# Row maxima of the second cross-attention: four heads at a time in row groups of the array, into one buffer of four banks

## The reference

```python
def _L1_xattn_ref(qkv, y):
    N_HEADS = 16
    bs, width, length = qkv.shape
    ch = width // N_HEADS
    q = qkv.reshape(bs * N_HEADS, ch, length)
    k = v = y.reshape(bs * N_HEADS, ch, -1)
    scale = 1.0 / math.sqrt(math.sqrt(ch))
    weight = jnp.einsum('bct,bcs->bts', q * scale, k * scale)
    weight = jax.nn.softmax(weight.astype(jnp.float32), axis=-1).astype(weight.dtype)
    a = jnp.einsum('bts,bcs->bct', weight, v)
    return a.reshape(bs, -1, length)
...
x = x + jnp.tanh(g_xattn[1]) * _L1_xattn_ref(_layernorm(x, axis=-1), ctx_2048)
```

## Time and profile before

| | |
|---|---|
| Median of three runs | 1993.25 us (1988.57 to 2001.61) |
| The profiled execution's own time | 1990.66 us |
| Its span, first to last instruction | 1988.8 us |
| Granted clock of TensorE, mean over the span | 0.926 of full speed |
| Busy in the span: TensorE matmuls, VectorE, ScalarE, GpSimd | 1719.1, 1290.5, 777.5, 829.1 us |
| Reductions of the maxima (L1257) | 512, 484.2 us |
| Matmuls of the maxima (L1383) | 1024, 315.0 us |

### The profile page before, as it was taken

How to read it: one execution, slowest core, us unless ns; L and a number is a source line. 1 busy time by engine, 2 the same in 40 slices (tenths; PEclk the granted TensorE clock), 3 DMA queues, 4 the chain that set the end, 5 groups by cost and what they waited for, 6 DMA issues and landing times. The chain is left out here.

```text
span 1988.8 us, 23904 instructions
## 1 busy us (share of the span) xinstructions
PE 1719.1 (86%) x8103; PEld 871.0 (44%) x8134; DVE 1290.5 (65%) x1649; ACT 777.5 (39%) x1275; POOL 829.1 (42%) x369
## 2 busy tenths in 40 slices
PE   5999999994656777899999998999999986989996
PEld 2444444442444543444444444444444323444443
DVE  3668989857898775766666665666666413565553
ACT  1211212113444533565655555655565554011010
POOL 0012222012554426577776676777767660000000
PEclk9999999996788876999999998999999996999999
DMA  8030312302000045143344444443332302000002
GB/s 320 9 114 20 89 44 66 124 34 82 1 0 0 0 104 142 39 105 92 87 98 105 105 105 106 105 94 78 89 86 70 71 1 87 1 0 0 0 0 85
DMA packets 83551, 137.19 MB, mean 69 GB/s; under 512 B 16606, under 2 KB 53490, under 8 KB 82678
## 3 DMA queue, kind: packets, MB, share of 16 engines
q1 hardware_dynamic: 83446, 135.84, 25.0%
HBM read 70.73 MB, written 8.66 MB: 40 GB/s over the span
## 5 line engine op out<-in xcount | busy, mean ns | idle before, releaser
L1257 DVE TENSOR_REDUCE c_piece_max<-c_unit 128x1 f32<-128x804 f32 x512 | 484.2, 990 | 280.4 <-PE c_unit L1383 277.1
L1342 ACT ACTIVATE c_prob<-c_scores 128x512 f32<-128x512 f32 (+1 forms) x832 | 472.2, 596 | 365.6 <-PE c_scores L1400 356.4
L1192 POOL TENSOR_TENSOR c_prob_sum<-c_prob_sum,c_prob 128x2048 f32<-128x2048 f32 x96 | 439.7, 4580 | 68.3 <-ACT c_prob L1342 64.3
L1400 PE MATMUL c_scores<-c_queries,c_keys 98*128 98x512 f32 (+1 forms) x832 | 358.1, 451 | 30.9 <-ACT c_prob L1342 16.6
L1383 PE MATMUL c_unit<-c_khigh,c_qdiag 128*128 128x402 f32 x1024 | 315.0, 393 | 23.3 <-DVE c_piece_max L1257 12.5
L1383 PEld LDWEIGHTS c_unit<-c_khigh,c_qdiag 128*128 128x128 f32 x1024 | 189.0, 204 | 175.9 <-DVE c_piece_max L1257 92.3
L1409 PE MATMUL c_out<-c_prob,c_VT 128*32 128x512 f32 (+1 forms) x1664 | 228.4, 629 | 22.1 <-issue 22.1
L1400 PEld LDWEIGHTS c_scores<-c_queries,c_keys 98*128 98x128 f32 (+1 forms) x832 | 158.0, 193 | 186.6 <-ACT c_prob L1342 132.3
L525 PE MATMUL a_S<-a_ctxT,a_xnT 128*128 128x401 f32 x512 | 188.9, 513 | 7.2 <-ACT a_prob L490 3.9
L555 PE MATMUL a_o<-a_ctx,a_probT 128*128 128x512 f32 (+1 forms) x416 | 181.2, 592 | 0.0
L1192 POOL TENSOR_TENSOR c_prob_sum<-c_prob 128x2048 f32<-128x2048 f32 x16 | 72.5, 4534 | 137.0 <-ACT c_prob L1342 137.0
(11 more groups left out here) (204 smaller groups left out, 2099.1 us busy)
## 6 DMA issues: line engine op xcount, KB each, us to landing
c_keys<-c_khigh SPq DMA_DIRECT2D x128, 200.2 KB, 3.0
c_k<-in_keys SPq DMA_DIRECT2D x16, 801.0 KB, 6.3
c_keys<-c_k SPq DMA_DIRECT2D x64, 200.2 KB, 3.0
a_ctx<-in_ctx SPq DMA_DIRECT2D x12, 1024.0 KB, 5.4
c_VT<-in_values SPq DMA_DIRECT2D x16, 768.0 KB
a_ctxT<-in_ctxT SPq DMA_DIRECT2D x12, 802.0 KB, 4.8
c_queries<-c_qhigh SPq DMA_DIRECT2D x128, 64.0 KB, 2.6
a_weights<-in_L_ffn_weight SPq DMA_DIRECT2D x3, 1408.0 KB, 13.6
```

Of the source, the lines that this page charges most:

```text
L1192: nc.gpsimd.tensor_tensor(psum4[:], a[:], prob[(j * MC + c) % RING][:], ALU.add).then_inc(sums_taken, 2 if i == 1 else 1)
L1257: nc.vector.tensor_reduce(piece_max[j % 2][:, k // 2, k % 2:k % 2 + 1], U[bank(unit)][:, :, 0:PIECE], axis=AX.XY, op=ALU.max).then_inc(uni ...
L1342: nc.scalar.activation(prob[(j * MC + c) % RING][0:w, h, :], STp[h % 2][0:w, :], ACT.Exp, scale=SCALE).then_inc(exp_done, 1)
L1400: nc.tensor.matmul(STp[h % 2][0:w, :], K[p][:, h, c * P:c * P + w].bitcast(F32R), Q[p][:, h, :].bitcast(F32R), start=True, stop=True).then ...
```

## The change

A unit of the maxima is now four matmuls, one for each head, for one group of 128 queries and one piece of 402 keys. Each works on the 32 partitions of its head with a `tile_position` in its own group of 32 rows of the array, and writes to its own bank. The unit fills all four banks, which before were two buffers of two, so the next unit may be issued only when VectorE has read this one. VectorE reduces 4 x 402 elements to four columns at once. A block has 16 units instead of 32 pairs (a stream of 17 with rows instead of 33), spread over the same 48 gaps. The zero-padded copies `QZ`, their fills on GpSimd, their transfers on SyncE's queue and the semaphore for them are gone; the matmuls read `qhigh` itself, so ScalarE's writing of `qhigh` for block n waits until the last unit of block n - 2 has been issued and done.

```diff
-        PAIRS = H * TB * 2
+        PIECES, PER = len(STARTS), H
+        PAIRS = H // PER * TB * PIECES
         UNITS = PAIRS + 1
-        AHEAD, ROWS_AT = PAIRS // 2, 8
+        AHEAD, ROWS_AT = PAIRS // 2, 4
...
-        QZ = [sb(f"c_qdiag{j}", [P, H, D]) for j in range(2)]
...
-        piece_max = [sb(f"c_piece_max{j}", [P, H * TB, 2]) for j in range(2)]
+        piece_max = [sb(f"c_piece_max{j}", [P, H, TB, PIECES]) for j in range(2)]
...
-        U = [ps(f"c_unit{j}", [P, 2, 512]) for j in range(2)]
+        U = ps("c_unit", [P, PER, 512])
...
-                if more:
-                    load_diagonal(g + 2, j % 2)
...
-            steps.link(pool.memset(QZ[0][:], 0.0))
...
-            steps.link(pool.memset(QZ[1][:], 0.0))
...
-                nc.vector.tensor_reduce(piece_max[j % 2][:, k // 2, k % 2:k % 2 + 1], U[bank(unit)][:, :, 0:PIECE], axis=AX.XY, op=ALU.max).then_inc(unit_read, 1)
+                h0, t, piece = part(k)
+                nc.vector.tensor_reduce(piece_max[j % 2][:, h0:h0 + PER, t, piece], U[:, :, 0:PIECE], axis=AX.X, op=ALU.max).then_inc(unit_read, 1)
...
-                    act.wait_ge(diag_loaded, (n - 1) * DIAGS)
+                    act.wait_ge(unit_full, FULL0 + place(n - 2, PAIRS - 1) + 1)
...
-                h, t, half, o = k // (2 * TB), k // 2 % TB, k % 2, j % 2
+                (h0, t, piece), o = part(k), j % 2
                 if k == 0:
-                    pe.wait_ge(diag_loaded, (n + 1) * DIAGS)
+                    pe.wait_ge(qhigh_ready, n + 1)
                     pe.wait_ge(khigh_ready, n + 1)
-                pe.wait_ge(unit_read, place(n, k) + 1)
-                for e in range(2):
-                    at = STARTS[2 * half + e]
-                    last = nc.tensor.matmul(U[bank(unit)][:, e, 0:PIECE], QZ[o][:, h, t * P:(t + 1) * P].bitcast(F32R), khigh[o][:, at:at + PIECE], start=True, stop=True)
+                pe.wait_ge(unit_read, place(n, k) + UNITS0)
+                at = STARTS[piece]
+                for e in range(PER):
+                    head = slice((h0 + e) * CH, (h0 + e + 1) * CH)
+                    last = nc.tensor.matmul(U[:, e, 0:PIECE], qhigh[o][head, t * P:(t + 1) * P], khigh[o][head, at:at + PIECE],
+                                            start=True, stop=True, tile_position=((h0 + e) * CH, 0))
                 last.then_inc(unit_full, 1)
```

More of the change, by code:

```diff
@@ L1023, in cross_attention_1 @@
         stacked = sem("c_stacked")
-        diag_loaded = sem("c_diag_loaded")
         unit_full = sem("c_unit_full")
@@ L1042, in cross_attention_1 @@
         FINS = 1
-        STACKS, ROWS, DIAGS = 16 * H * 6, 16 * H, 16 * H
+        STACKS, ROWS = 16 * H * 6, 16 * H
         EXPS0, PV0, UNITS0, FULL0, SCORES0 = 2, RING, 2, 1, 1
@@ L1087, in unit_stream, with part @@
             return stream
[L1089 to L1094, removed]
+        def part(k):
+            return k // (TB * PIECES) * PER, k // PIECES % TB, k % PIECES
         block = stack.enter_context(nc.Block())
@@ L1106, in load_values @@
                 sp.dma_start(VT[j][0:ML, MC - 1, :], src[:, (MC - 1) * P:M, :].rearrange("o p k -> p (o k)")).then_inc(v_loaded[j], 16)
[L1108 to L1114, removed]
             load_keys(0, 0)
             load_keys(1, 1)
-            sp.wait_ge(consts_ready, 3)
-            load_diagonal(0, 0)
-            sp.wait_ge(consts_ready, 4)
             def slot(g, j, main, nxt, more, later):
@@ L1260, in maximum @@
                     dve.wait_ge(unit_read, UNITS0 + place(n, k) + 1)
-                    nc.vector.tensor_reduce(nmax[:].rearrange("p h t -> p (h t)"), piece_max[j % 2][:], axis=AX.X, op=ALU.max, negate=True).then_inc(nmax_ready, 1)
+                    nc.vector.tensor_reduce(nmax[:], piece_max[j % 2][:], axis=AX.X, op=ALU.max, negate=True).then_inc(nmax_ready, 1)
             def keep_rows(unit):
@@ L1266, in keep_rows @@
                 dve.wait_ge(unit_full, FULL0 + rows_place(n) + 1)
-                nc.vector.tensor_copy(nrow[:], U[bank(unit)][0:2 * H, 0, :]).then_inc(unit_read, 1)
+                nc.vector.tensor_copy(nrow[:], U[0:2 * H, 0, :]).then_inc(unit_read, 1)
                 dve.wait_ge(unit_read, UNITS0 + rows_place(n) + 1)
@@ L1388, in rows @@
                 pe.wait_ge(nparts_ready, n + 1)
-                pe.wait_ge(unit_read, rows_place(n) + 1)
+                pe.wait_ge(unit_read, rows_place(n) + UNITS0)
                 for t in range(TB):
-                    last = nc.tensor.transpose(U[bank(unit)][0:2 * H, 0, t * P:(t + 1) * P], nparts[:, t, :, :].rearrange("p h a -> p (h a)"), ident[:])
+                    last = nc.tensor.transpose(U[0:2 * H, 0, t * P:(t + 1) * P], nparts[:, t, :, :].rearrange("p h a -> p (h a)"), ident[:])
                 last.then_inc(unit_full, 1)
@@ L1436, in slot @@
                         rows(unit) if unit[0] == "rows" else pair(unit)
-                    pe.wait_ge(consts_ready, 7)
+                    pe.wait_ge(consts_ready, 5)
                     for h in range(H):
```

## The result

The change made the kernel slower: median 2099.2 us (2094.27 to 2102.86) against 1992.7, a ratio of 1.053 (95% interval 1.048 to 1.057). The forecast was 2014 us: slower, as measured, but by a fifth of the measured step. The profiled execution has a span of 2099.1 us against 1988.8, 110 more.

What follows compares the result with a forecast made beforehand. TensorE's in-order queue was taken as the bound. 5 (prologue) + 3 (block 0's slot) + 13 slots x (0.3 + 0.8) + 0.5 (slot 14) = 22.8 us on 1990.66 gave 2013.5, with the median's offset 2014 us; range 1955 to 2070.

Steps and rivals of the forecast that it cites:

- Order and bound: Second cross-attention blocks: TensorE's in-order queue is the bound, busy 49.2 of 52.6 us a block at 2.4 GHz.
- Four matmuls in row groups: Units of the maxima: four matmuls overlap in 0.2 us, about 0.4 us from unit to next score with mode changes.
- The rival in which they don't overlap: Units' four matmuls hold 0.74 us, every interval grows by 0.54, 9 us a block, 2162 us in all; chance 0.08.
- The single buffer: Maxima's buffer: TensorE must wait for VectorE's read, so at least 2.44 us from unit to unit, setting eight intervals a block.
- The walk through a block: Sum of the intervals from unit to unit in one block at full clock: 52.9 us, against 52.6 before.
- The clock: Turns of the blocks: longer idle brings two stretches at low clock at nearly every turn, another 0.8 us a block.
- The rival with the clock: Blocks: units with idle between them leave the clock low longer, two further stretches a block, 2046 us; chance 0.17.
- the 57 that the prediction named as a sign of being wrong: Reciprocals, one a block: expected 53 to 55 us apart; under 51 or over 57 would show the forecast wrong.
- Block 0's slot: Slot of block 0, 24 intervals instead of 48 pairs: 64.2 us against 62.2 before, with a slow start +3.
- The prologue: Block 0's units at 1.2 GHz: 2.7 us each, start 2.2 us earlier, the rest of the maxima 5 us later.
- The rival "no price for the change of mode": Weight loads stay hidden: unit holds 0.25, scores around it 0.23, 49.2 us a block, 1964 us in all; chance 0.19.

Runs made afterwards that it cites:

- the gaps filled: The changed kernel with whole-array matmuls added between two scores, or a score and a unit, that had nothing between them: 2084 us, ratio 1.042 to before.
- the padded units on the single buffer: The changed kernel with zero-padded copies over all 128 rows in place of row groups, four-bank single buffer kept: 2144 us, ratio 1.076 to before.
- the run with two heads: The changed kernel with row groups kept but two heads a unit, 32 units, into two buffers of two banks: 2089 us, ratio 1.044 to before.
- the run with seven: The changed kernel with each unit's four matmuls issued seven times over into the same banks: ratio 1.164 to before, 70.7 us a block.

## Why the prediction was wrong

**Order and bound** held: TensorE's queue is still the busiest (83% of the span), and VectorE, GpSimd and ScalarE have the busy time per block that they had the earlier trace rows.

**Four matmuls in row groups** held. I took 0.4 us from unit to score, and it is 0.38. The rival in which they don't overlap is out.

**The single buffer** held: 2.40 us from unit to unit against 2.44.

**The walk through a block** was 1.8 us short. At full clock the 13 intervals from the fourth on take 38.9 us by the starts of their reductions, where I had 37.1. With my figures for the other four that makes 54.7 us a block against 52.9. Two terms were too small. The score between two modes holds 0.43 in place of 0.34 or 0.33. The larger one is the loop through ScalarE, 1.18 us for two scores, which the walk charged only in "s s s out". It also sets "s s out s" (2.87 us against 2.44), the interval behind the rows (1209.40 to 1213.20, so 3.80 against 3.12) and "s s den sum out s" (1218.81 to 1223.40, so 4.59 against 4.15), three intervals that make some 1.5 of the 1.8 us, about 1.3 of it by scores that wait for an exponential. In "s s out s" the third row starts 1.19 us after the first:

```profile
1189.59 0.73 PE L1384 MATMUL c_scores<-c_queries,c_keys 98*128 98x512 f32 x2
1190.25 0.45 PE L1366 MATMUL c_unit<-c_khigh,c_qhigh 32*128 32x402 f32 x4
1190.78 0.98 PE L1384 MATMUL c_scores<-c_queries,c_keys 98*128 98x512 f32 x2
1191.70 1.06 PE L1393 MATMUL c_out<-c_prob,c_VT 128*32 128x512 f32 x8
1192.69 0.49 PE L1384 MATMUL c_scores<-c_queries,c_keys 98*128 98x512 f32 x1
1193.12 0.46 PE L1366 MATMUL c_unit<-c_khigh,c_qhigh 32*128 32x402 f32 x4
```

The comparison that made me trust the walk could not have shown this: the 3.22 us "measured" are 1255.84 to 1259.06, the same rows from which its prices were read, so the sum had to come out. These reductions open and close the stretch of 38.9 us (timeline of VectorE, after), and its row by engine follows:

```profile
1185.04 1.83 DVE L1239 TENSOR_REDUCE c_piece_max<-c_unit 128x4 f32<-128x1608 f32 x1 [0.59 <-PE c_unit L1366]
...
1223.91 1.83 DVE L1239 TENSOR_REDUCE c_piece_max<-c_unit 128x4 f32<-128x1608 f32 x1 [2.76 <-PE c_unit L1366]
...
1185.04:1223.91 38.87, 34.57 (x210) 11.76 (x210) 23.74 (x17) 20.71 (x38) 26.73 (x11) 1.00 0.09 19
```

**The clock** is the step that failed: "another 0.8 a block". I let the low clock come only at the turns, as a longer version of the dips of before. Slots 1 to 13 now take 60.7 us a block on average, 6.0 over the 54.7 at full clock, where before it was 54.3 over 52.6, 1.7. So by this sum the clock costs 4.3 us a block more, not 0.8. The 54.7 are in part my estimate; the 56.1 us of a block at full clock with matmuls added bound it from above, so that it is at least 2.9 more. Even the 0.8 was read too small: it is the mean over 15 intervals, and the last two, with half a stream or none, are short (48.8 and 46.5 us) and hid the dips of the full slots, which cost 1.7.

In the changed kernel the clock falls in the middle of blocks too, here 32 us behind the reciprocal at 920.3, after a stretch in which TensorE waited for an exponential (0.45 us) and a reduction (0.41):

```profile
949.00:952.40 3.40, 2.54 (x20) 1.01 (x12) 2.38 (x3) 1.80 (x4) 3.32 (x2) 1.00 0.00 0
952.40:955.80 3.40, 3.40 (x17) 0.66 (x17) 2.20 (x3) 0.60 (x1) 1.44 (x1) 0.54 0.00 0
```

And TensorE goes on waiting at the low clock. Two units after a turn (a score holds 0.72):

```profile
1050.34 1.22 PE L1384 MATMUL c_scores<-c_queries,c_keys 98*128 98x512 f32 x2
1051.82 0.79 PE L1384 MATMUL c_scores<-c_queries,c_keys 98*128 98x512 f32 x1 [0.26 <-ACT c_prob L1324]
1052.54 0.71 PE L1366 MATMUL c_unit<-c_khigh,c_qhigh 32*128 32x402 f32 x4
1053.18 0.79 PE L1384 MATMUL c_scores<-c_queries,c_keys 98*128 98x512 f32 x1
```

The rival with the clock named the mechanism and its row (the prologue's 35 us at the low level), but sized it at two more stretches a block and gave it 0.17. The row should have had more weight: it showed pairs and waits in turn, as the change makes of the whole stage. The reciprocals stand 58 to 63 us apart up to slot 13, past the 57 that the prediction named as a sign of being wrong.

**Block 0's slot** has the lowest clock: 84.3 us from its first unit (776.12) to the reciprocal, at 0.66, against 62.2 at 0.98. I had priced 3 us for it, and it is 22. At least 7 of it are the clock's: with the gaps filled the slot takes 77.3 us at 0.81 (778.63 to 855.90), added work included. The rest is not separated from the buffer's waits; the padded units on the single buffer take 84.7 us for the slot at 0.85 (793.58 to 878.30). **The prologue** was right by its parts: a unit every 2.65 us (2.7 forecast), and the rest of the maxima 1 us later than before instead of 5, since the first unit started 4.5 us earlier (720.58; 2.2 forecast).

```profile
720.58 0.71 PE L1366 MATMUL c_unit<-c_khigh,c_qhigh 32*128 32x402 f32 x4 [8.20 <-ACT c_khigh L1296]
723.22 0.71 PE L1366 MATMUL c_unit<-c_khigh,c_qhigh 32*128 32x402 f32 x4 [1.94 <-DVE c_piece_max L1239]
...
776.12 0.71 PE L1366 MATMUL c_unit<-c_khigh,c_qhigh 32*128 32x402 f32 x4
```

The sum by these terms: 13 x (2.1 + 4.3) = 83 for slots 1 to 13, of which I had 14; 22 for block 0's slot, of which I had 3; 5 for the last two, of which I had 0.5; 1 at the start, of which I had 5. That is 111 of the 110 us measured.

Three readings of the prediction were off by little: 2013.5 and the 2.6 us of the median make 2016, not 2014; by its rows out comes 6.73 us behind the last unit at the turn (5.81 + 1.83 - 0.91), not 6.65, and the trace after has 6.59 (1223.40 to 1229.99); and 1.3 us for a further stretch at the low clock is the first dip of its rows, where the second adds 0.5.

**The rival "no price for the change of mode"** is out: a score behind a unit holds 0.34 (the first of the two at 1196.49, 0.74 less the 0.40 of one) and one between two modes 0.43, not 0.23. Of the Trainium skill's two rules, the first ("TensorE: Matmul & The Clock Gate", Part 3) agrees with the trace: four at once take little more than one. The estimate of 0.24 us by its figure was high: each further four in a visit adds 0.19. The second ("TensorEngine Tiling (Array Packing)", Key Properties), the drain at a change of mode, agrees in sign: the scores next to a change hold 0.1 us more on each side, drain and unhidden weight load together.

## What to carry to other kernels

The change bought cheaper matmuls with a buffer, and lost on both sides. The single buffer alone cost more than row groups can save here (6.6 us a block against 3.5 by the prediction's walk), and the cheaper matmuls left less work between the waits, with which the clock went. When a change trades TensorE's work for waits, price the whole stage at both clock levels, and look for a stretch of the trace where work and waits already alternate as they will. Where TensorE has a known wait, a few matmuls into a bank that nobody reads can pay for themselves: 0.8% on the kernel before, with one wait of 1.7 us a block filled.

## What the runs showed of the hardware

- Adding work made the kernel faster: 43 us less with some 490 more matmul records in the stage (2056 against 2099 us, ratios to before 1.029 and 1.053), and 18 less on the kernel before with 112 (1979 against 1998 in the same comparison).
- Four matmuls in row groups end 0.45 us after the unit's start, as two do (the run with two heads); repeating the four costs 0.19 us each time (1.50 us held with seven, 0.38 with one), where four whole-array matmuls hold 0.74.
- The granted clock did not follow the busy share of the rows: 0.96 at 85% busy with padded units, 0.88 at 96% with two heads in row groups.

```profile
1101.60 1.57 PE L1366 MATMUL c_unit<-c_khigh,c_qhigh 32*128 32x402 f32 x28 [0.32 <-DVE c_piece_max L1239]
1103.10 0.50 PE L1384 MATMUL c_scores<-c_queries,c_keys 98*128 98x512 f32 x1
...
1105.25 0.45 PE L1372 MATMUL c_unit<-c_khigh,c_qhigh 32*128 32x402 f32 x2
```

The first two rows are of the run with seven, the last of the run with two heads.
